# GpSimd's queue issues part and table loads in an attention stage, and the stage's fills stand in another order

## The chip, the core and the metric

The kernel runs on one core of a Trainium2 chip. The core has TensorE (PE; its weight loads are listed as PEld), VectorE (DVE), ScalarE (ACT), GpSimd (POOL) and SyncE (SP), each with an instruction stream of its own. The streams meet only at semaphores. The metric is the device time of one execution in microseconds, median of several; lower is better.

## What is computed

The reference is a network of four layers on x of 16 x 256 tokens with 128 features: linear attention, a mixture of eight experts, disentangled attention, and the experts again. The change touches the third layer, the disentangled attention with 16 heads of 8 features:

```python
scores = jnp.einsum('bhsd,bhkd->bhsk', q, k) / jnp.sqrt(jnp.float32(hd * 3))
c2p = jnp.einsum('bhsd,hkd->bhsk', q, pos_k)
c2p = jnp.take_along_axis(c2p, jnp.clip(rel + span, 0, 2 * span - 1)[None, None], axis=-1)
scores = scores + c2p / bias_scale
p2c = jnp.einsum('bhsd,hkd->bhsk', k, pos_q)
p2c = jnp.take_along_axis(p2c, jnp.clip(-rel + span, 0, 2 * span - 1)[None, None], axis=-1)
scores = scores + p2c.swapaxes(-1, -2) / bias_scale
ctx = jnp.einsum('bhsk,bhkd->bhsd', jax.nn.softmax(scores, axis=-1), v)
```

## The kernel before

`attend` computes this attention. Its work is cut into 32 **units**: one head and one half of the batch (8 entries of 256 x 256 scores). A unit has eight **steps**, one for each batch entry. While a unit's scores are made, the position terms (c2p and p2c) of the next unit are computed too; these are the **fills**, ten for each unit, listed in `FILLS`, and `SHARE` says how many of them stand in each step. Heads 0 and 15 are written out, the 14 between are a loop. I count units from 0 to 31; unit 31 has no fills. Unit 30 loads no tables and no rows, since there is no head 16.

In a step b, in the order of each stream:

- TensorE: `qk` of entry b (L1340), `t2`, the transposes of entry b - 3 (L1351), in the fourth and eighth step `av` (L1362), in the first and fifth `back` (L1369), then the step's fills. Fills: staged ("c2p", L1296, 16 matmul passes), pair (L1332), near (L1323), far (L1305), edge (L1313).
- ScalarE: in the first and fifth step `values` (L1446), then the exponentials of entry b - 3 (L1451), then it copies the step's fills out of PSUM: staged ones by two copies into `STAGE` (L1415), near and edge ones by L1427, pairs by L1434.
- VectorE: the sum of position terms (L1503), the subtraction of the maximum for half of entry b - 1 (L1517), the scores with their maximum (L1510), in the first and fifth step the `results` (L1495, L1498), and the copy of a far fill (L1487).
- GpSimd: the other half of the subtraction (L1266), which `t2` needs too.

A staged fill does not go straight to its place. SyncE copies it from `STAGE` to the tile `CT` by three DMAs, a **spread set** (L1222 twice, L1226 once). `STAGE` holds two fills, so the copy of staged fill 2 waits until the spread set of fill 0 has landed, and fill 3 waits for set 1. VectorE starts a unit when all fills are copied and all four sets have landed.

SyncE also loads for coming units: **parts** (`load_parts`: q once, L1209, k three times, L1211, table ends once, L1212, into a buffer of the next unit; far and edge fills and `qk` read them), **tables** (`load_tables`, L1198, two DMAs) and **rows** (`load_rows`, L1204, 16 small DMAs). The tables and rows loaded in a unit are read by the fills of the next unit. All of it stands in one queue and is issued in the order written. PSUM banks of the fills alternate between two; a fill waits until the fill two banks earlier has been copied out.

## Time and profile before

| | us |
|---|---|
| median of 3 runs | 1508.21 (1508.12 to 1508.65) |
| profiled execution, time | 1508.99 |
| its span, first to last instruction | 1507.0 |
| TensorE / VectorE / ScalarE / GpSimd busy | 1018.8 / 886.6 / 665.2 / 491.6 |
| units, first add of unit 0 to the last score | about 434 to 1293 |

A row of the timeline gives the start in us, the time it took, engine, line, operation, the tiles out<-in, how many instructions are merged, and in brackets how long the engine stood idle before it and what ended the wait. `SPq` is SyncE issuing a DMA; the time in its row is that of the issue, not of the transfer. "granted clock" (PEclk) is TensorE's clock as a share of 2.4 GHz. Busy time of an engine does not bound this stage by itself; what matters is who waits for whom in a unit.

### The profile page before, as it was taken

How to read it: one execution, taken by the hardware profiler on the slowest of the kernel's cores; microseconds unless marked ns; L12 is line 12 of the kernel's file. 1: busy time of each engine (PE TensorE's matmuls, PEld its weight loads, DVE VectorE, ACT ScalarE, POOL GpSimd, SP SyncE). 2: the span in 40 equal slices, each digit the busy share in tenths (PEclk: the TensorE clock that was granted, in tenths of full speed). 3: DMA queues.
4: the chain of work that ended last, by engine and by line, in shares of the span. 5: the costliest groups of instructions: out<-in, count | busy, mean ns of one | idle time of the engine just before them, and what ended most of it. 6: DMA issues, size and time to landing. Idle time of an engine off the chain costs nothing. (4 is left out here: it accounts for less than half of the span.)

```text
span 1507.0 us, 32133 instructions
## 1 busy us (share of the span) xinstructions
PE 1018.8 (68%) x8740; PEld 753.3 (50%) x8740; DVE 886.6 (59%) x2997; ACT 665.2 (44%) x1563; POOL 491.6 (33%) x504
## 2 busy tenths in 40 slices
PE   4892438856257767777677677776777768760876
PEld 3881327754035545455455454554554545560776
DVE  6888635556436656656556555565565656644555
ACT  2237114434435545555455455554554556310443
POOL 3305037531033323323323223232332333203664
PEclk8995559986668988989889889898898999755999
DMA  6900333330765544544444545444454454014331
GB/s 152 212 1 1 126 97 117 95 91 35 270 148 117 122 129 110 128 116 126 123 116 126 123 117 125 116 125 123 111 132 118 119 129 103 1 49 137 103 100 48
DMA packets 113730, 167.21 MB, mean 111 GB/s; under 512 B 16361, under 2 KB 68656, under 8 KB 113168
## 3 DMA queue, kind: packets, MB, share of 16 engines
q1 hardware_dynamic: 108048, 153.93, 40.1%
q0 software_dynamic: 5632, 12.70, 2.4%
q8 instruction: 21, 0.34, 0.1%
q14 instruction: 29, 0.24, 0.1%
HBM read 64.96 MB, written 35.55 MB: 67 GB/s over the span
## 5 line engine op out<-in xcount | busy, mean ns | idle before, releaser
L1266 POOL TENSOR_SCALAR ds_p2c<-ds_p2c,ds_max 128x256 f32<-128x256 f32 x256 | 270.7, 1058 | 576.1 <-DVE ds_max L1510 576.1
L1510 DVE CUSTOM_DVE_ANT_0 ds_p2c<-ds_bank,ds_p2c 128x256 f32<-128x256 f32 x512 | 196.1, 419 | 129.8 <-PE ds_bank L1340 128.9
L1415 ACT ACTIVATE ds_stage<-ds_bank 128x512 f32<-128x512 f32 x256 | 138.9, 595 | 267.4 <-PE ds_bank L1296 142.2
L1296 PE MATMUL ds_bank<-ds_tab,d_qkr 64*64 64x256 f32 x2048 | 176.0, 465 | 57.2 <-DMA d_qkr<-scratch_qk 37.2
L1503 DVE TENSOR_TENSOR ds_p2c<-ds_c2p,ds_p2c 128x512 f32<-128x512 f32 x256 | 184.1, 719 | 42.7 <-ACT ds_p2c L1427 28.6
L1351 PE MATMUL ds_bank<-all_constants,ds_p2c 128*128 128x128 f32 x1024 | 170.8, 293 | 2.9 <-ACT all_xt L1451 1.6
L1451 ACT ACTIVATE all_xt<-ds_bank 128x512 f32<-128x512 f32 x256 | 153.4, 599 | 37.6 <-PE ds_bank L1351 37.4
L1296 PEld LDWEIGHTS ds_bank<-ds_tab,d_qkr 64*64 64x64 f32 x2048 | 101.4, 199 | 105.8 <-issue 76.7
L1351 PEld LDWEIGHTS ds_bank<-all_constants,ds_p2c 128*128 128x128 f32 x1024 | 136.3, 155 | 9.9 <-issue 2.3
L1434 ACT ACTIVATE ds_p2c<-ds_bank 128x256 f32<-128x256 f32 x256 | 77.5, 390 | 114.8 <-PE ds_bank L1332 114.6
L1369 PE MATMUL ds_bank<-all_constants,ds_values_t 128*128 128x128 f32 x128 | 29.4, 313 | 142.1 <-ACT ds_values_t L1446 142.1
L1332 PE MATMUL ds_bank<-d_qkr,ds_tab 64*128 64x128 f32 x1024 | 101.9, 356 | 32.5 <-DVE ds_p2c L1487 32.3
L1517 DVE TENSOR_SCALAR ds_p2c<-ds_p2c,ds_max 128x256 f32<-128x256 f32 x256 | 116.8, 456 | 0.0
L1340 PE MATMUL ds_bank<-ds_ks,ds_qs 72*128 72x256 bf16 x512 | 111.8, 305 | 4.2 <-DVE ds_max L1510 4.2
L1332 PEld LDWEIGHTS ds_bank<-d_qkr,ds_tab 64*128 64x128 f32 x1024 | 86.7, 251 | 52.3 <-DVE ds_p2c L1487 41.0
L1369 PEld LDWEIGHTS ds_bank<-all_constants,ds_values_t 128*128 128x128 f32 x128 | 13.3, 146 | 158.3 <-ACT ds_values_t L1446 158.3
L1487 DVE COPY ds_p2c<-ds_bank 128x512 f32<-128x512 f32 x64 | 44.1, 688 | 75.2 <-PE ds_bank L1305 75.2
L1427 ACT ACTIVATE ds_p2c<-ds_bank 64x512 f32<-64x512 f32 x128 | 75.8, 592 | 28.3 <-PE ds_bank L1313 21.4
L1495 DVE RECIPROCAL ds_rec<-ds_bank 128x8 f32<-128x8 f32 x64 | 13.1, 205 | 119.2 <-PE ds_bank L1369 119.2
L453 ACT ACTIVATE 0fe_h<-0fe_bank,0fe_expert 128x128 f32<-128x128 f32 x160 | 45.6, 368 | 80.0 <-PE 0fe_bank L414 80.0
L453 ACT ACTIVATE 1fe_h<-1fe_bank,1fe_expert 128x128 f32<-128x128 f32 x160 | 45.6, 368 | 79.2 <-PE 1fe_bank L414 79.2
L1340 PEld LDWEIGHTS ds_bank<-ds_ks,ds_qs 72*128 72x128 bf16 x512 | 32.7, 100 | 81.2 <-issue 58.3
(274 smaller groups left out, 1820.0 us busy)
## 6 DMA issues: line engine op xcount, KB each, us to landing
ds_c2p<-ds_stage SPq DMA_DIRECT2D x256, 128.0 KB
ds_c2p<-ds_stage SPq DMA_DIRECT2D x128, 256.0 KB
slots_in<-all_zero SPq DMA_DIRECT2D x2, 5180.0 KB, 38.2
ds_qs<-scratch_q_parts SPq DMA_DIRECT2D x32, 288.0 KB
ds_ks<-scratch_k_parts SPq DMA_DIRECT2D x96, 96.0 KB
d_qkr<-scratch_qk SPq DMA_DIRECT2D x512, 8.0 KB
ds_tab<-scratch_tables SPq DMA_DIRECT2D x32, 248.0 KB, 3.7
ds_tab<-scratch_tables SPq DMA_DIRECT2D x32, 195.5 KB, 3.2
```

The lines of the kernel that those rows point to most:

```text
L453: act.activation(h[i % 2][:, c, :], ph[i % 2][:, c * P:(c + 1) * P], ACT.Gelu_apprx_tanh, bias=WB[i][:, B1_AT + c:B1_AT + c + 1]).then_inc ...
L1266: pool.tensor_scalar(PC[half][:, 1, b, :], PC[half][:, 1, b, :], mx[:, 2 * b + 1:2 * b + 2], None, ALU.subtract).then_inc(s_sub1, 1)
L1296: last = pe.matmul(pc[swap][to * 64:(to + 1) * 64, st * SEQ:(st + 1) * SEQ], own, TAB[half][rows, 0, c:c + SEQ], start=True, stop=True)
L1332: last = pe.matmul(pb[tile][:, :].rearrange("p (r a n) -> p r a n", r=2, a=4)[:, :, a, :], TAB[half][rows, kind, c:c + P], own, start=True ...
L1340: last = pe.matmul(pqk[b % 2][:, st * SEQ:(st + 1) * SEQ], QS[half][:, b * SEQ + st * P:b * SEQ + (st + 1) * P], KS[half][:, b * SEQ:(b + ...
L1351: last = pe.transpose(pt2[:, kt * SEQ + st * P:kt * SEQ + (st + 1) * P], PC[half][:, st, b, kt * P:(kt + 1) * P], con["ident"])
L1415: act.activation(STAGE[:, 2 * (where % 2) + swap, :], pc[swap][:, :], ACT.Copy).then_inc(s_cc, 1)
L1434: last = act.activation(dst, pb[tile][:, side * 256:(side + 1) * 256].rearrange("p (g s b) -> p g b s", g=4, b=HALF), ACT.Copy)
L1451: act.activation(PT[b], pt2[:, :].rearrange("p (k s) -> p k s", k=2), ACT.Exp).then_inc(s_exp, 1)
L1503: dve.tensor_tensor(z, CT[half][:, b, :, :], z, ALU.add).then_inc(s_z, 1)
L1510: last = dve.tensor_tensor_reduce(out=PC[half][:, st, b, :], in0=pqk[b % 2][:, st * SEQ:(st + 1) * SEQ], in1=PC[half][:, st, b, :], scale= ...
L1517: dve.tensor_scalar(PC[half][:, 0, b, :], PC[half][:, 0, b, :], mx[:, 2 * b:2 * b + 1], None, ALU.subtract).then_inc(s_sub0, 1)
```

## The change

Three things. GpSimd's queue issues parts and tables instead of SyncE's: the five part loads after its first subtraction of a unit, the two table loads after its fourth, with the two waits that SyncE had before them; at the start of the stage GpSimd issues the first tables and parts. SyncE's rows are no longer dealt four to each spread set but 5, 0, 9 and 2. And `FILLS` and `SHARE` are changed: staged fills in steps one, two, five and six, a pair in step three, the near fill in step four, a far fill and a pair in step seven, a far fill and the edge fill in step eight. (`own` asks for a semaphore named with the stage's full prefix; `ds` has no digit to strip, so the names stay what they were.)

```diff
-        s_rows, s_ct, s_tab, s_stack = ([m.sem(f"{n}{i}") for i in range(2)] for n in ("rows", "c2p", "tab", "stack"))
+        s_rows, s_ct, s_tab, s_stack = ([m.sem(f"{n}{i}", own=n in ("tab", "stack")) for i in range(2)] for n in ("rows", "c2p", "tab", "stack"))
...
-        FILLS = [CROSS[0], CROSS[1], NEAR, CROSS[2], FARS[0], PAIRS[0], CROSS[3], PAIRS[1], FARS[1], EDGE]
+        FILLS = [CROSS[0], CROSS[1], PAIRS[0], NEAR, CROSS[2], CROSS[3], FARS[0], PAIRS[1], FARS[1], EDGE]
...
-        SHARE = [1, 1, 1, 1, 2, 1, 2, 1]
+        SHARE = [1, 1, 1, 1, 1, 1, 2, 2]
...
-                    if not (last and half == 1):
-                        sp.wait_ge(s_sc, HALF * u + 2)
-                        sp.sem_inc(s_go_sp, 1)
-                        load_parts(*following(head, half))
+                    sp.wait_ge(s_sc, HALF * u + 2)
+                    sp.sem_inc(s_go_sp, 1)
                     if not last:
                         sp.wait_ge(s_bm, BM * (u + 1))
                         sp.sem_inc(s_go_sp, 1)
                         sp.wait_ge(s_cm, CM * (u + 1))
                         sp.sem_inc(s_go_sp, 1)
-                        load_tables(head + 1, half)
-                    for i in range(len(CROSS)):
+                    for i, count in enumerate((5, 0, 9, 2)):
                         if not last:
-                            load_rows(head + 1, half, 4 * i, 4)
+                            load_rows(head + 1, half, (0, 5, 5, 14)[i], count)
                         if not (last and half == 1):
                             spread(*following(head, half), i)
...
                         pool.tensor_scalar(PC[half][:, 1, b, :], PC[half][:, 1, b, :], mx[:, 2 * b + 1:2 * b + 2], None,
                                            ALU.subtract).then_inc(s_sub1, 1)
-
+                        if b == 0 and not (last and half == 1):
+                            load_parts(*following(head, half))
+                        if b == 3 and not last:
+                            pool.wait_ge(s_bm, BM * (u + 1))
+                            pool.sem_inc(s_go_pool, 1)
+                            pool.wait_ge(s_cm, CM * (u + 1))
+                            pool.sem_inc(s_go_pool, 1)
+                            load_tables(head + 1, half)
+
+            load_tables(0, 0)
+            load_parts(0, 0)
+            load_tables(0, 1)
             pool.wait_ge(s_bo, 16)
```

How it moves the instructions, at the three places that matter. First SyncE's queue in the second unit (head 0, second half), before; `ds_qs`, `ds_ks` and `ds_ends` are the parts, `ds_tab` the tables, `d_qkr` the rows, `ds_c2p` the spreads:

```order
L1209 DMA ds_qs<-scratch_q_parts 72x1x2048
L1211 DMA ds_ks<-scratch_k_parts 24x2048 x3
L1212 DMA ds_ends<-scratch_far_f 72x1x256
L1198 DMA ds_tab<-scratch_tables 128x1x391
L1198 DMA ds_tab<-scratch_tables 128x1x496
L1204 DMA d_qkr<-scratch_qk 8x2x128 x4
L1222 DMA ds_c2p<-ds_stage 8x8x512 x2
L1226 DMA ds_c2p<-ds_stage 16x8x512
```

The same queue and unit in the changed kernel:

```order
L1200 DMA d_qkr<-scratch_qk 8x2x128 x5
L1211 DMA ds_c2p<-ds_stage 8x8x512 x2
L1215 DMA ds_c2p<-ds_stage 16x8x512
L1211 DMA ds_c2p<-ds_stage 8x8x512 x2
L1215 DMA ds_c2p<-ds_stage 16x8x512
L1200 DMA d_qkr<-scratch_qk 8x2x128 x9
```

Seven loads no longer stand before the first spread set, and five small row loads do. Next GpSimd's stream in that unit, changed kernel; before, there are eight subtractions in a row here and nothing else:

```order
L1261 TENSOR_SCALAR ds_p2c1<-ds_p2c1,ds_max 128x256 [waits ds_scores]
L1250 DMA ds_qs0<-scratch_q_parts 72x1x2048
L1252 DMA ds_ks0<-scratch_k_parts 24x2048 x3
L1253 DMA ds_ends0<-scratch_far_f 72x1x256
L1261 TENSOR_SCALAR ds_p2c1<-ds_p2c1,ds_max 128x256 [waits ds_scores] x3
L1246 DMA ds_tab1<-scratch_tables 128x1x391 [waits ds_bias_mm,ds_c2p_mm]
L1246 DMA ds_tab1<-scratch_tables 128x1x496
L1261 TENSOR_SCALAR ds_p2c1<-ds_p2c1,ds_max 128x256 [waits ds_scores] x4
```

The second subtraction now stands behind five DMA issues, the fifth behind two more. Last TensorE's stream, fourth to sixth step of the second unit (each step begins with L1340), before:

```order
L1340 MATMUL ds_bank<-ds_ks,ds_qs 128x256 x2
L1351 MATMUL ds_bank<-all_constants,ds_p2c 128x128 x4
L1362 MATMUL ds_bank<-all_xt,ds_head_v 32x256 x8
L1296 MATMUL ds_bank<-ds_tab,d_qkr 64x256 x8
L1340 MATMUL ds_bank<-ds_ks,ds_qs 128x256 x2
L1351 MATMUL ds_bank<-all_constants,ds_p2c 128x128 x4
L1369 MATMUL ds_bank<-all_constants,ds_values_t 128x128 x2
L1305 MATMUL ds_bank<-ds_ks,ds_ends 128x512
L1332 MATMUL ds_bank<-d_qkr,ds_tab 128x2x64 x8
L1340 MATMUL ds_bank<-ds_ks,ds_qs 128x256 x2
L1351 MATMUL ds_bank<-all_constants,ds_p2c 128x128 x4
L1296 MATMUL ds_bank<-ds_tab,d_qkr 64x256 x8
```

and in the changed kernel:

```order
L1346 MATMUL ds_bank<-ds_ks,ds_qs 128x256 x2
L1357 MATMUL ds_bank<-all_constants,ds_p2c 128x128 x4
L1368 MATMUL ds_bank<-all_xt,ds_head_v 32x256 x8
L1329 MATMUL ds_bank<-d_qkr,ds_tab 64x128 x8
L1346 MATMUL ds_bank<-ds_ks,ds_qs 128x256 x2
L1357 MATMUL ds_bank<-all_constants,ds_p2c 128x128 x4
L1375 MATMUL ds_bank<-all_constants,ds_values_t 128x128 x2
L1302 MATMUL ds_bank<-ds_tab,d_qkr 64x256 x8
L1346 MATMUL ds_bank<-ds_ks,ds_qs 128x256 x2
L1357 MATMUL ds_bank<-all_constants,ds_p2c 128x128 x4
L1302 MATMUL ds_bank<-ds_tab,d_qkr 64x256 x8
```

Staged fill 2 (before in the fourth step) moved to the fifth, the far and the pair fill left the fifth step, and the near fill stands in the fourth.

## Rows read from the trace of the kernel before

**Rows 1.** The page, busy time of one engine, its share and instructions.

```profile
PE 1018.8 (68%) x8740; PEld 753.3 (50%) x8740; DVE 886.6 (59%) x2997; ACT 665.2 (44%) x1563; POOL 491.6 (33%) x504
```

**Rows 2.** The list of waits: who waited for whom, us, times, longest.

```profile
ACT ds_stage L1415 <- DMA ds_c2p<-ds_stage: 125.2, 30, 5.0
```

**Rows 3.** The timeline of SyncE's queue, 850 to 905 us.

```profile
872.63 0.87 SPq L1209 DMA_DIRECT2D ds_qs<-scratch_q_parts  x1
...
876.45 1.36 SPq L1198 DMA_DIRECT2D ds_tab<-scratch_tables  x2
878.00 1.79 SPq L1204 DMA_DIRECT2D d_qkr<-scratch_qk  x4
...
881.67 0.58 SPq L1226 DMA_DIRECT2D ds_c2p<-ds_stage  x1
```

**Rows 4.** The timeline of all engines, 881 to 889 us: where they wait.

```profile
885.79 1.08 ACT L1415 ACTIVATE ds_stage<-ds_bank 128x512 f32<-128x512 f32 x2 [4.52 <-DMA ds_c2p<-ds_stage]
...
887.21 0.44 PE L1369 MATMUL ds_bank<-all_constants,ds_values_t 128*128 128x128 f32 x2 [4.05 <-ACT ds_values_t L1446]
...
887.68 0.21 DVE L1495 RECIPROCAL ds_rec<-ds_bank 128x8 f32<-128x8 f32 x1 [4.02 <-PE ds_bank L1369]
```

**Rows 5.** The timeline: first adds of units 0, 1, 30 and 31.

```profile
434.06 0.69 DVE L1503 TENSOR_TENSOR ds_p2c<-ds_c2p,ds_p2c 128x512 f32<-128x512 f32 x1 [5.87 <-DMA ds_c2p<-ds_stage]
...
465.14 0.69 DVE L1503 TENSOR_TENSOR ds_p2c<-ds_c2p,ds_p2c 128x512 f32<-128x512 f32 x1 [1.11 <-DMA ds_c2p<-ds_stage]
...
1255.58 0.69 DVE L1503 TENSOR_TENSOR ds_p2c<-ds_c2p,ds_p2c 128x512 f32<-128x512 f32 x1 [0.95 <-ACT ds_p2c L1427]
...
1277.52 0.69 DVE L1503 TENSOR_TENSOR ds_p2c<-ds_c2p,ds_p2c 128x512 f32<-128x512 f32 x1 [1.11 <-DMA ds_c2p<-ds_stage]
```

**Rows 6.** The timeline of all engines in unit 30, 1253 to 1281 us.

```profile
1256.38 1.16 PE L1296 MATMUL ds_bank<-ds_tab,d_qkr 64*64 64x256 f32 x16
...
1257.46 0.92 POOL L1266 TENSOR_SCALAR ds_p2c<-ds_p2c,ds_max 128x256 f32<-128x256 f32 x1 [1.70 <-DVE ds_max L1510]
...
1258.97 1.16 PE L1296 MATMUL ds_bank<-ds_tab,d_qkr 64*64 64x256 f32 x16 [0.67 <-ACT ds_stage L1415]
...
1260.07 0.39 PE L1340 MATMUL ds_bank<-ds_ks,ds_qs 72*128 72x256 bf16 x2
...
1264.69 0.39 PE L1340 MATMUL ds_bank<-ds_ks,ds_qs 72*128 72x256 bf16 x2
...
1264.98 1.08 ACT L1415 ACTIVATE ds_stage<-ds_bank 128x512 f32<-128x512 f32 x2 [1.33 <-PE ds_bank L1296]
...
1265.61 0.42 DVE L1510 CUSTOM_DVE_ANT_0 ds_p2c<-ds_bank,ds_p2c 128x256 f32<-128x256 f32 x1
...
1266.39 0.44 PE L1369 MATMUL ds_bank<-all_constants,ds_values_t 128*128 128x128 f32 x2 [0.87 <-ACT ds_values_t L1446]
...
1267.25 0.68 DVE L1487 COPY ds_p2c<-ds_bank 128x512 f32<-128x512 f32 x1
...
1268.08 1.16 PE L1332 MATMUL ds_bank<-d_qkr,ds_tab 64*128 64x128 f32 x16 [1.03 <-DVE ds_p2c L1487]
...
1273.33 0.56 SPq L1226 DMA_DIRECT2D ds_c2p<-ds_stage  x1
...
1273.92 0.38 PE L1340 MATMUL ds_bank<-ds_ks,ds_qs 72*128 72x256 bf16 x2
...
1275.67 0.41 PE L1313 MATMUL ds_bank<-ds_ks,ds_ends 72*64 72x512 bf16 x2
```

**Rows 7.** Busy time by stretch: engines in turn, granted clock, DMA share, GB/s.

```profile
861.00:867.00 6.00, 5.63 (x40) 3.86 (x41) 3.05 (x9) 1.90 (x6) 1.19 (x1) 0.50 0.44 101
1255.58:1277.52 21.94, 17.52 (x200) 12.00 (x200) 16.19 (x55) 14.19 (x32) 8.63 (x9) 1.00 0.56 125
```

**Rows 8.** DMA issues on GpSimd: one in the timeline, and L347's min/median/max.

```profile
190.79 0.96 POOL L353 DMA_INDIRECT slots_in<-all_rows,0f_slot  x1 [0.30 <-issue]
...
L347 POOL DMA_INDIRECT tokens<-0fe_y,0fe_token x40: 969/1156/1559, 224.7 to 327.2; - x40
```

More of the change, by code:

```diff
@@ L1195, in _ @@
         def _(sp):
-            def load_tables(head, half):
-                for j in range(2):
-                    sp.dma_start(TAB[half][:, j, 0:(TABLE_Q, TABLE)[j]], views["tables"][j][:, bass.ds(head * DB, DB), :]).then_inc(s_tab[half], 16)
             def load_rows(head, half, first, count):
@@ L1205, in load_rows @@
                                  dram["qk"][:, bass.ds(head * DB, DB), half * HT + at.start:half * HT + at.stop].rearrange("j p n -> p j n")).then_inc(s_rows[half], 16)
-            def load_parts(head, half):
-                rows, cols = bass.ds(head * 3 * DB, 3 * DB), slice(half * HT, (half + 1) * HT)
-                sp.dma_start(QS[half][:, :], views["q_parts"][rows, :, cols]).then_inc(s_stack[half], 16)
-                for i in range(3):
-                    sp.dma_start(KS[half][i * 3 * DB:(i + 1) * 3 * DB, :], views["k_parts"][rows, cols]).then_inc(s_stack[half], 16)
-                sp.dma_start(ENDS[half][:, :], views["far_f"][rows, :, :]).then_inc(s_stack[half], 16)
             def spread(head, half, i):
@@ L1239, in heads @@
                         sp.sem_inc(s_go_sp, 1)
-                        load_tables(head + 1, half)
-                    for i in range(len(CROSS)):
+                    for i, count in enumerate((5, 0, 9, 2)):
                         if not last:
-                            load_rows(head + 1, half, 4 * i, 4)
+                            load_rows(head + 1, half, (0, 5, 5, 14)[i], count)
                         if not (last and half == 1):
                             spread(*following(head, half), i)
-            load_tables(0, 0)
             load_rows(0, 0, 0, 16)
-            load_parts(0, 0)
             for i in range(len(CROSS)):
                 spread(0, 0, i)
-            load_tables(0, 1)
             load_rows(0, 1, 0, 16)
@@ L1260, in _, with load_tables, load_parts @@
         def _(pool):
+            def load_tables(head, half):
+                for j in range(2):
+                    pool.dma_start(TAB[half][:, j, 0:(TABLE_Q, TABLE)[j]], views["tables"][j][:, bass.ds(head * DB, DB), :]).then_inc(s_tab[half], 16)
+            def load_parts(head, half):
+                rows, cols = bass.ds(head * 3 * DB, 3 * DB), slice(half * HT, (half + 1) * HT)
+                pool.dma_start(QS[half][:, :], views["q_parts"][rows, :, cols]).then_inc(s_stack[half], 16)
+                for i in range(3):
+                    pool.dma_start(KS[half][i * 3 * DB:(i + 1) * 3 * DB, :], views["k_parts"][rows, cols]).then_inc(s_stack[half], 16)
+                pool.dma_start(ENDS[half][:, :], views["far_f"][rows, :, :]).then_inc(s_stack[half], 16)
             def heads(head, last):
                 for half in range(2):
+                    u = 2 * head + half
                     for b in range(HALF):
```

## The prediction

> **What bounds the kernel now.** I read the shares first: TensorE is the busiest engine and still idle for a third of the span [rows 1], so the time is in waits. In the list of waits, GpSimd's idle time costs nothing (it is waiting for work); the one that matters is ScalarE's staged copy L1415, which waits 125.2 us in 30 places for a DMA, `ds_c2p<-ds_stage` [rows 2]. Thirty places is once a unit. A unit is eight steps, and its start is best seen at VectorE's first add (L1503): 465.14 for unit 1 and 1255.58 for unit 30, so (1255.58 - 465.14) / 29 = 27.26 us a unit [rows 5].
>
> Then one unit in order of time. SyncE's queue starts it at 872.63 with five loads of parts, two of tables at 876.45 and four of rows at 878.00; only then come the spreads of staged fill 0, the third of them at 881.67 [rows 3]. Staged fill 2 uses the same staging rows, so its copy waits for that landing: it starts at 885.79 after 4.52 us idle. ScalarE takes its work in order, and behind that copy stand `values` and the exponentials; TensorE therefore idles 4.05 us before L1369, VectorE 4.02 us before L1495 [rows 4]. After such a gap TensorE's clock is granted at 0.50 for some microseconds, that is at 1.2 instead of 2.4 GHz [rows 7].
>
> Unit 30 is the trial that the old kernel already holds. SyncE has parts to load there but no tables and no rows. Its staged copy 2 (1264.98) shows no wait, the clock is 1.00 throughout [rows 6, 7], and the unit lasts 1277.52 - 1255.58 = 21.94 us [rows 5], 5.32 us less. The difference of TensorE's waits before L1369 (4.05 against 0.87) explains 3.18 of it [rows 4, 6]; the other 2.14 I put down to the low clock.
>
> **What the change takes from SyncE.** Parts and tables go from 872.63 to 878.00: 5.4 us of SyncE's queue in each unit [rows 3]. What stays is 16 row loads, about 0.43 us each (four and their gaps end at about 879.8), and four spread sets of 2.1 us. Counting from the unit's first add as 0, SyncE is free at -0.9, five row loads end at 1.3, and spread set 0 goes out when its copy is ready, as in unit 30; so no load stands before a spread that is ready. From a set's third DMA to its landing takes 4.1 to 4.2 us (881.67 to 885.79; 1273.33 to 1277.52) [rows 3, 5, 6]. Set 0 lands near 8.5, set 1 near 11.
>
> **What the new fill order does.** Staged copies 2 and 3 come in the fifth and sixth step, the far and edge fills, which need the parts, in the last two. I lay the unit out from the spacings of unit 30 [rows 6], again from its first add. To the fifth step the work is as long as before (a pair fill replaces a near fill and a near fill a staged one: the same size within 0.1 us). L1369 runs at 1266.39 - 1255.58 = 10.8, staged fill 2 at 11.3. From a staged fill to the next, whose bank must be copied out, 1258.97 - 1256.38 = 2.6: fill 3 at 13.9. From there to the next `qk` 1.1 (1258.97 to 1260.07): 15.0. From a `qk` to the end of VectorE's scores 1.3 (1264.69 to 1266.0): 16.3. Only now can VectorE copy the far fill out (0.69, L1487), and the pair fill behind it waits for that bank, as it does at 1268.08: about 17.1. Then `qk` of the last step at 18.2, the edge fill 1.75 later (1273.92 to 1275.67) plus 0.4 for the far fill that now stands before it: 20.35; and from the edge fill to the next unit's first add 1.85 (1275.67 to 1277.52): **22.2 us**. So the new order in itself is no faster than unit 30's; it makes room for late parts.
>
> The last spread set gets little room in this. Staged copy 3 is ready from 15.8; SyncE has two row loads before the set, its third DMA is issued near 17.7 and lands near 21.9, 0.3 us before it is needed. Tables and rows are in flight beside it, so I add 0.3 us.
>
> **What it costs on GpSimd.** No row shows a plain load issued by GpSimd. Bounds: an undisturbed indirect issue takes 0.96 us with 0.30 before it, 1.26 a piece; beside VectorE's copies it takes up to 1.56, with 0.30 that is 1.86 [rows 8]. A plain load has no list of addresses to read and three of the five have only 24 rows, so it could also be cheaper; below 1.26 nothing changes, as follows. GpSimd's first subtraction ends at 1257.46 + 0.92 - 1255.58 = 2.8 [rows 6]. Behind it are now five issues of pitch p, and behind them the subtraction of entry 1, which transpose L1351 needs in the fifth step, at about 9.3 (qk at 9.1). It gets it at 3.9 + 5p, and with the transposes (0.6) and L1369 (0.5) staged fill 2 starts at 5.0 + 5p. The plan above has 11.3. So the unit grows by 5p - 6.3: nothing at p = 1.26, 0.7 at 1.4, 1.7 at 1.6, 3.0 at 1.86. I take p = 1.4, the undisturbed issue plus a third of what the disturbance can add, since VectorE's in-SBUF subtraction fills about that share of a step. The later subtractions have slack again (entry 3 is done near 14, wanted at 15.2), and the two table issues after it (2.8 us) end near 17, with the tables wanted at 23; GpSimd's load is 8.6 us in a unit [rows 7] plus 7 x 1.4 = 18.4 of 23. The waits at the fourth entry (`s_bm`, `s_cm`) count fills of the unit before and are met when they are reached.
>
> **The sum.** 22.2 + 0.7 + 0.3 = 23.2 us a unit against 27.26: 4.06 x 29 units = 118 us. Unit 30 has no stall to lose and gets the GpSimd term, +1. Start and unit 0 (434.06 to 465.14 [rows 5]): tables leave SyncE twice, some 2.5 us, and the five issues stand behind GpSimd's bias add, which costs about as much back; I put -1. The profiled execution took 1508.99 (span 1507.0), 0.8 above the median 1508.21; its parts fit the median to 0.05%. Forecast 1508.2 - 118 = **1390 us**.
>
> **Two rules of the skill.** The rows show SyncE's issues as the cause of the stall. The Trainium skill (DMA: Bandwidth & Descriptors, "Issuing engines are not separate DMA queues") says that a second issuing engine saves only sequencer time, usually small beside the transfer; by that the time stays at 1508, which is rival 4. Unit 30 speaks against it here: 5.32 us follow from issue time.
> The rows show an issue on GpSimd growing from 0.97 to 1.56 us beside VectorE's copies [rows 8]. The Trainium skill (SBUF — State Buffer, "SBUF: two separate sides") says that GpSimd can't write descriptors while VectorE runs a two-port operation; the direction agrees with the trace. What it would do at its full length here is rival 3.
>
> **Rivals.**
> 1. The last spread set decides. It stands 0.3 us from the bound by the plan; if tables, parts and a denser stream of transfers (DMA share 0.56 in unit 30 without tables and rows [rows 7]) delay its landing by 1 to 2 us, the unit is 24.2 to 25.2: 1419 to 1448. For it: spacing; against: the transfers are also spread over two queues. 12 in 100.
> 2. GpSimd is late but the clock stays. Each issue meets one of VectorE's subtractions, p 1.6 to 1.8: unit 24.2 to 25, 1419 to 1443. 8 in 100.
> 3. **Slower: GpSimd late and the clock falls.** TensorE's wait for entry 1 is 3.9 + 5p - 9.3. At p = 1.86 it is 3.9 us, about the gap of 4.05 after which the clock is low today, while the waits of 1.03 in unit 30 left it at 1.00 [rows 4, 6, 7]. The low clock adds 2.1: 22.2 + 3.0 + 2.1 = 27.3, where the kernel is today. Above p = 1.86 it is slower; at 2.2 the unit is 22.2 + 4.7 + 2.1 = 29.0, +50 us, 1559. 6 in 100.
> 4. The change does not do what it says: the stall stays or another of its size takes its place, within 0.2% of 1508. 3 in 100.
> 5. Issues cheap, landing in time: unit 22.0 to 22.4, 1360 to 1367. 8 in 100.
>
> **How the numbers follow.** The forecast's own case, p from 1.26 to 1.6, is a unit of 22.4 to 24.2: 1367 to 1419, 63 in 100. With the faster case and the two late ones the range is 1358 to 1445. 0.2% (3 us) is what a measurement of this kernel can tell. Faster 0.91 (63 + 12 + 8 + 8), within 0.2% 0.03, slower 0.06.
>
> **What the changed profile would show.** Right: a first add every 23 us; no row of L1415 waiting for `ds_c2p<-ds_stage`; granted clock 1.00 through the units; GpSimd issues of 0.9 to 1.3 us, with L1351 waiting under 2 us once a unit. Wrong: waits of L1351 for GpSimd of over 3 us, the clock at 0.50 in each unit, or L1503 waiting for the DMA `ds_c2p<-ds_stage` for over 1 us at each unit's start.

## The result and the profile after

| | before | changed kernel |
|---|---|---|
| median, us | 1508.16 (1507.77 to 1508.65, 4 runs) | 1408.13 (1400.51 to 1416.35, 4 runs) |
| ratio | | 0.9338, 95% interval 0.9277 to 0.9398 |
| span of the profiled execution | 1507.0 | 1410.7 |
| TensorE's granted clock, mean | 0.829 | 0.867 |
| mean of units 1 to 29 | 27.26 | 23.75 |

The kernel is 100 us faster; 118 were forecast. The page's busy line, the answer to [rows 1], shows as many instructions on TensorE and VectorE as before, TensorE done with them sooner since its clock is higher, and 118 us more on GpSimd:

```profile
PE 980.5 (70%) x8740; PEld 719.6 (51%) x8740; DVE 889.5 (63%) x2997; ACT 661.3 (47%) x1563; POOL 610.1 (43%) x728
```

The list of waits (who waited for whom: us, times, longest), the answer to [rows 2]. The staged copy now stands on L1421 and still waits for spread sets, and VectorE's first add of a unit (L1509) waits for them too:

```profile
DVE ds_p2c L1509 <- DMA ds_c2p<-ds_stage: 86.7, 30, 5.1
ACT ds_stage L1421 <- DMA ds_c2p<-ds_stage: 72.6, 28, 4.5
```

First adds of units 0, 1, 8, 9, 16, 17, 30 and 31 in VectorE's timeline, the answer to [rows 5]:

```profile
439.53 0.69 DVE L1509 TENSOR_TENSOR ds_p2c<-ds_c2p,ds_p2c 128x512 f32<-128x512 f32 x1 [2.78 <-DMA ds_c2p<-ds_stage]
...
470.93 0.69 DVE L1509 TENSOR_TENSOR ds_p2c<-ds_c2p,ds_p2c 128x512 f32<-128x512 f32 x1 [4.33 <-DMA ds_c2p<-ds_stage]
...
639.18 0.69 DVE L1509 TENSOR_TENSOR ds_p2c<-ds_c2p,ds_p2c 128x512 f32<-128x512 f32 x1 [1.13 <-DMA ds_c2p<-ds_stage]
...
666.92 0.69 DVE L1509 TENSOR_TENSOR ds_p2c<-ds_c2p,ds_p2c 128x512 f32<-128x512 f32 x1 [1.13 <-ACT ds_p2c L1433]
...
828.85 0.69 DVE L1509 TENSOR_TENSOR ds_p2c<-ds_c2p,ds_p2c 128x512 f32<-128x512 f32 x1 [4.09 <-DMA ds_c2p<-ds_stage]
...
850.94 0.69 DVE L1509 TENSOR_TENSOR ds_p2c<-ds_c2p,ds_p2c 128x512 f32<-128x512 f32 x1 [1.34 <-DMA ds_c2p<-ds_stage]
...
1159.81 0.69 DVE L1509 TENSOR_TENSOR ds_p2c<-ds_c2p,ds_p2c 128x512 f32<-128x512 f32 x1 [1.84 <-DMA ds_c2p<-ds_stage]
...
1181.55 0.69 DVE L1509 TENSOR_TENSOR ds_p2c<-ds_c2p,ds_p2c 128x512 f32<-128x512 f32 x1 [1.84 <-DMA ds_c2p<-ds_stage]
```

The difference of the two traces closes with these rows. Units 1 to 29 take 688.9 us instead of 790.4 (-101.6), unit 0 begins 5.5 us later, unit 0 itself is 0.3 longer, unit 30 is 0.2 shorter, and what follows the start of unit 31 is 0.3 shorter: -96.3, the difference of the spans.

The units are of two kinds, which a mean hides. Eighteen of the 29 take 22.0 to 23.3 us (mean 22.5), unit 16 among them with 850.94 - 828.85 = 22.09. Eleven take 24.3 to 27.7 (mean 25.8), such as unit 8 with 27.74. Had all been of the first kind, the kernel would be 11 x 3.3 = 36 us faster.

Unit 8 in the timelines of SyncE's queue, GpSimd, ScalarE and TensorE, the answer to [rows 3] and [rows 4]:

```profile
641.72 1.28 SPq L1211 DMA_DIRECT2D ds_c2p<-ds_stage  x2
...
642.00 0.62 POOL L1250 DMA_DIRECT2D ds_qs<-scratch_q_parts  x1
...
642.62 1.58 POOL L1252 DMA_DIRECT2D ds_ks<-scratch_k_parts  x3
...
643.18 0.56 SPq L1215 DMA_DIRECT2D ds_c2p<-ds_stage  x1
...
644.16 0.66 POOL L1253 DMA_DIRECT2D ds_ends<-scratch_far_f  x1
...
644.20 2.29 SPq L1211 DMA_DIRECT2D ds_c2p<-ds_stage  x2
...
647.46 4.13 SPq L1200 DMA_DIRECT2D d_qkr<-scratch_qk  x9
...
647.96 1.13 POOL L1246 DMA_DIRECT2D ds_tab<-scratch_tables  x2
...
653.74 1.09 ACT L1421 ACTIVATE ds_stage<-ds_bank 128x512 f32<-128x512 f32 x2 [3.69 <-DMA ds_c2p<-ds_stage]
...
654.97 1.98 PE L1302 MATMUL ds_bank<-ds_tab,d_qkr 64*64 64x256 f32 x16 [3.07 <-ACT ds_stage L1421]
...
657.38 1.08 ACT L1421 ACTIVATE ds_stage<-ds_bank 128x512 f32<-128x512 f32 x2 [2.07 <-DMA ds_c2p<-ds_stage]
```

Spread set 0 is issued beside the parts, set 1 and then the tables and nine rows beside each other. Set 0's third DMA is issued at 643.18 and the copy that waits for it starts at 653.74: 10.6 us, where it was 4.1 before. TensorE waits 3.07 us behind that copy, and its clock falls to 0.50: staged fill 3 takes 1.98 us, the same 16 matmuls 1.16 at full clock [rows 6]. Windows over this stretch (PE, PEld, DVE, ACT and POOL busy, granted clock, DMA share, GB/s) show what the landing met. The DMA share adds up the times of all packets that start in a window, over 16 engines (so a window can pass 1); it stands at 0.81 to 1.07 until set 0 has landed:

```profile
643.00:645.00 2.00, 2.00 (x30) 1.50 (x23) 2.00 (x9) 1.48 (x3) 2.00 (x5) 1.00 0.81 191
645.00:647.00 2.00, 2.00 (x30) 1.11 (x26) 2.00 (x7) 1.79 (x6) 2.00 (x2) 1.00 0.96 163
647.00:649.00 2.00, 1.81 (x26) 1.39 (x22) 1.16 (x5) 0.89 (x2) 2.00 (x4) 1.00 0.93 154
649.00:651.00 2.00, 1.39 (x18) 0.96 (x18) 1.09 (x5) 1.04 (x3) 1.01 (x2) 1.00 1.07 189
651.00:653.00 2.00, 0.90 (x10) 0.58 (x6) 1.90 (x8) 0.00 (x0) 0.38 (x1) 1.00 0.89 184
...
655.00:657.00 2.00, 2.00 (x17) 0.94 (x18) 0.00 (x0) 0.31 (x1) 0.00 (x0) 0.50 0.47 146
```

Before, the ten microseconds from 876 to 886 of unit 16 had a share of 0.56.

What separates the two kinds is the moment at which set 0 leaves. GpSimd issues the parts 2.8 us after a unit's first add (5.5 in unit 17). In seventeen of the eighteen short units set 0's third DMA is out 0.7 to 2.5 us after the first add, ahead of the parts, and by the times at which the trace counts up its semaphore it lands 4.1 to 4.4 us later, as forecast. In the long ones it is out at 3.2 to 4.9 and takes 6.8 to 10.5 us (unit 17: 4.1). Short unit 26 is the border case, 3.1 and 6.9. VectorE's wait at the first add goes with it: 2.1 to 5.1 us in short units, 1.1 to 1.9 in long ones. While VectorE waits there, TensorE and ScalarE get ahead, and set 0 is out sooner after the first add (wait and issue add up to 5.1 us in unit 8 and in unit 16).

### The profile page after: what moved, and what is told of

Its sections match the earlier page's. It is cut to its first block and busy times, and to the rows that moved or that the text cites. A ratio compares the mean times of both kernels' runs of the same rounds, so it can differ in the third digit from the quotient of the medians.

```text
span 1410.7 us, 32238 instructions
## 1 busy us (share of the span) xinstructions
PE 980.5 (70%) x8740; PEld 719.6 (51%) x8740; DVE 889.5 (63%) x2997; ACT 661.3 (47%) x1563; POOL 610.1 (43%) x728
## 5 line engine op out<-in xcount | busy, mean ns | idle before, releaser
L1261 POOL TENSOR_SCALAR ds_p2c<-ds_p2c,ds_max 128x256 f32<-128x256 f32 x256 | 265.9, 1042 | 360.8 <-DVE ds_max L1516 359.7
L1509 DVE TENSOR_TENSOR ds_p2c<-ds_c2p,ds_p2c 128x512 f32<-128x512 f32 x256 | 187.2, 731 | 89.0 <-DMA ds_c2p<-ds_stage 86.7
L1421 ACT ACTIVATE ds_stage<-ds_bank 128x512 f32<-128x512 f32 x256 | 139.0, 595 | 211.3 <-PE ds_bank L1302 138.6
L1302 PE MATMUL ds_bank<-ds_tab,d_qkr 64*64 64x256 f32 x2048 | 156.5, 421 | 88.2 <-ACT ds_stage L1421 51.6
L1357 PE MATMUL ds_bank<-all_constants,ds_p2c 128*128 128x128 f32 x1024 | 164.6, 285 | 9.0 <-ACT all_xt L1457 6.4
L1357 PEld LDWEIGHTS ds_bank<-all_constants,ds_p2c 128*128 128x128 f32 x1024 | 125.4, 148 | 19.8 <-issue 9.7
L1523 DVE TENSOR_SCALAR ds_p2c<-ds_p2c,ds_max 128x256 f32<-128x256 f32 x256 | 114.8, 448 | 0.0
L1346 PE MATMUL ds_bank<-ds_ks,ds_qs 72*128 72x256 bf16 x512 | 105.0, 288 | 11.5 <-DVE ds_max L1516 11.4
L1338 PE MATMUL ds_bank<-d_qkr,ds_tab 64*128 64x128 f32 x1024 | 79.8, 299 | 27.2 <-DVE ds_p2c L1493 27.2
L1338 PEld LDWEIGHTS ds_bank<-d_qkr,ds_tab 64*128 64x128 f32 x1024 | 66.9, 199 | 44.9 <-DVE ds_p2c L1493 33.5
L1368 PE MATMUL ds_bank<-all_xt,ds_head_v 128*32 128x256 f32 x1024 | 77.9, 428 | 0.7 <-ACT all_xt L1457 0.7
L353 POOL DMA_INDIRECT slots_in<-all_rows,1f_slot x32 | 31.6, 986 | 87.7 <-POOLq L176 78.2
L347 POOL DMA_INDIRECT tokens<-0fe_y,0fe_token x40 | 46.3, 1158 | 51.2 <-DVE 0fe_y L485 45.5
```

The costliest lines, as they stand in the source:

```text
L1261: pool.tensor_scalar(PC[half][:, 1, b, :], PC[half][:, 1, b, :], mx[:, 2 * b + 1:2 * b + 2], None, ALU.subtract).then_inc(s_sub1, 1)
L1302: last = pe.matmul(pc[swap][to * 64:(to + 1) * 64, st * SEQ:(st + 1) * SEQ], own, TAB[half][rows, 0, c:c + SEQ], start=True, stop=True)
L1338: last = pe.matmul(pb[tile][:, :].rearrange("p (r a n) -> p r a n", r=2, a=4)[:, :, a, :], TAB[half][rows, kind, c:c + P], own, start=True ...
L1346: last = pe.matmul(pqk[b % 2][:, st * SEQ:(st + 1) * SEQ], QS[half][:, b * SEQ + st * P:b * SEQ + (st + 1) * P], KS[half][:, b * SEQ:(b + ...
L1357: last = pe.transpose(pt2[:, kt * SEQ + st * P:kt * SEQ + (st + 1) * P], PC[half][:, st, b, kt * P:(kt + 1) * P], con["ident"])
L1368: last = pe.matmul(pu[j * VG:(j + 1) * VG, :], VH[half][:, 2 * (4 * part + j) + kt, :], PT[4 * part + j][:, kt, :], start=(kt == 0), stop= ...
```

## The experiments

All times are medians; each ratio is against runs of the kernel before that were taken beside it. "New order" is the changed kernel's `FILLS` and `SHARE`. Of the twelve expectations three held with their range (the rows' deal, staged fill 2 alone, and the last one); the other nine times lie outside every range that was written down for them, so these show directions and not prices.

**One part alone.** First the new order, with SyncE issuing everything as before and the rows dealt four by four:

```diff
-        FILLS = [CROSS[0], CROSS[1], NEAR, CROSS[2], FARS[0], PAIRS[0], CROSS[3], PAIRS[1], FARS[1], EDGE]
+        FILLS = [CROSS[0], CROSS[1], PAIRS[0], NEAR, CROSS[2], CROSS[3], FARS[0], PAIRS[1], FARS[1], EDGE]
-        SHARE = [1, 1, 1, 1, 2, 1, 2, 1]
+        SHARE = [1, 1, 1, 1, 1, 1, 2, 2]
```

> Only the order of the fills and the steps they stand in is changed; SyncE issues parts, tables and rows as before. Theory A (what is left of the stall in the changed kernel is late landings of spread sets, since their transfers share the DMA engines with parts and tables): SyncE's queue still puts set 0 out at 8.1 us of a unit, it lands at 12.3, and staged copy 2 is now wanted only at 12.6, so the old stall goes by the order alone; set 1 lands at 16.3 (wanted 15.1) and set 3 near 24.5, so a unit is 24.8 to 25.3 us, 29 x 2.2 = 64 us less than before, about 1440 to 1450. Rival B (it is the moved issue work that removes the stall, the order alone does little): a unit stays above 26.5, over 1485.

Measured: **1369.1** us, ratio 0.9058 (0.9023 to 0.9094), units of 22.5. That is more than the whole gain of the change: the order alone is 39 us faster than order and queue together. Then the reverse, the changed kernel with the old `FILLS` and `SHARE`:

> GpSimd issues parts and tables and the rows are dealt 5, 0, 9, 2, but the fills stand in the old order. Theory A: staged copy 2 is wanted at 9.4 us of a unit while set 0 lands later than that beside the parts (6 to 10 us after its issue), and the far fill in step five wants parts at 11.3 that land near 14; a unit is 25 to 27 us, 1445 to 1505. Rival B: freeing SyncE's queue is enough, a unit is 22 to 23 as in unit 30, about 1370.

Measured: **1561.6**, ratio 1.0339 (1.0281 to 1.0397): slower than before. Its list of waits has the old stall, only longer (125.2 us in [rows 2]):

```profile
ACT ds_stage L1421 <- DMA ds_c2p<-ds_stage: 168.4, 30, 6.8
```

Both rivals fell with these two: that the moved issue work is what removes the stall, and that freeing SyncE's queue is enough. Theory A comes nearer in both, but it put the new order at least 71 us too slow, and the old one with GpSimd's queue at least 57 us too fast and on the wrong side of the kernel before.

**Issues or bytes.** The changed kernel, with parts of 16 columns and tables of 8 from the second head on: as many DMAs and as many issues, hardly any bytes. The other columns are left out of the computation.

```diff
+                w_, e_ = (HT, 2 * FAR) if first else (16, 16)
-                pool.dma_start(QS[half][:, :], views["q_parts"][rows, :, cols]).then_inc(s_stack[half], 16)
+                pool.dma_start(QS[half][:, 0:w_], views["q_parts"][rows, :, cols]).then_inc(s_stack[half], 16)
```

> The changed kernel, but from the second head on the part and table loads that GpSimd issues carry only the first 8 to 16 columns (same number of DMAs and rows, almost no bytes; later heads compute on stale data). Theory A: with the bytes gone the spread sets land 4 us after their issue, staged copies 2 and 3 wait for no DMA, the low clock goes; the wait of VectorE at a unit's start shrinks from 2.9 to 1 us or less; a unit is 22.3 to 22.8, about 1365 to 1380. Rival C (the price is GpSimd's issue work or the number of its transfers, not their bytes): 23.5 or more, within 10 us of 1408.

Measured: **1346.8**, ratio 0.8931 (0.8903 to 0.8960), units of 21.6. ScalarE's wait for spread sets is gone from the list; one remains:

```profile
DVE ds_p2c L1512 <- DMA ds_c2p<-ds_stage: 64.7, 32, 2.8
```

So the bytes of parts and tables cost the changed kernel 61 us. Their issue on GpSimd costs next to nothing: in this kernel TensorE waited for a subtraction of GpSimd once, 0.6 us, and in the changed kernel never.

**The moment.** Parts after GpSimd's third subtraction instead of the first, tables after the sixth:

> The changed kernel with the parts issued after GpSimd's third subtraction instead of its first, and the tables after the sixth instead of the fourth. Theory A: spread sets 0 and 1 leave alone and land 4 us after issue, no wait of staged copy 2, fewer units with the low clock, a unit 22.5 to 23.2, about 1375 to 1395. Against it: the parts' last load landed 8.9 us after its issue in the changed kernel (median); issued at about 9 it would reach the first far fill, wanted at 15.8, 2 us late, and set 3 meets the tables: 24 to 25 us, 1415 to 1445.

Measured: **1512.7**, ratio 1.0024 (1.0007 to 1.0041). The parts now come too late for the far fill, once in every unit:

```profile
PE ds_bank L1311 <- DMA ds_ends<-scratch_far_f: 103.4, 31, 3.9
```

The other way: GpSimd issues parts and tables ahead of its first subtraction, as soon as SyncE used to:

```diff
+                    pool.wait_ge(s_sc, HALF * u + 2)
+                    if not (last and half == 1):
+                        load_parts(*following(head, half))
+                    if not last:
+                        pool.wait_ge(s_bm, BM * (u + 1))
+                        pool.wait_ge(s_cm, CM * (u + 1))
+                        load_tables(head + 1, half)
                     for b in range(HALF):
...
-                        if b == 0 and not (last and half == 1):
-                            load_parts(*following(head, half))
-                        if b == 3 and not last:
...
-                            load_tables(head + 1, half)
```

> The changed kernel, but GpSimd issues a unit's parts and tables ahead of its first subtraction (parts once two scores of the unit are there, tables right behind), where SyncE issued them, instead of after the first and after the fourth subtraction: parts some 5 us and tables some 8 us earlier, in front of spread sets 0 and 1 rather than beside them. Theory T (the moment: parts and tables fly at the same time as the spread sets): the sets land in 4 to 5 us again, units of 22 to 22.7 us, 1365 to 1380. Theory S (the software queue is itself the slow or greedy one, wherever it is issued): most of the 39 us stay, 1392 to 1415.

Measured: **1354.3**, ratio 0.8986 (0.8962 to 0.9010): the fastest kernel of the study that computes everything, 54 us ahead of the changed kernel, with units of 21.8. It also beats the new order alone, by 15 us, so with the right moment the second queue does pay. Unit 16 in the timelines of GpSimd, VectorE, SyncE's queue and ScalarE:

```profile
792.86 0.64 POOL L1250 DMA_DIRECT2D ds_qs<-scratch_q_parts  x1 [0.31 <-issue]
...
794.79 0.69 DVE L1511 TENSOR_TENSOR ds_p2c<-ds_c2p,ds_p2c 128x512 f32<-128x512 f32 x1 [1.82 <-DMA ds_c2p<-ds_stage]
...
796.15 1.14 POOL L1246 DMA_DIRECT2D ds_tab<-scratch_tables  x2 [0.29 <-PE ds_bank L1304]
...
798.10 0.56 SPq L1215 DMA_DIRECT2D ds_c2p<-ds_stage  x1
...
806.21 1.08 ACT L1423 ACTIVATE ds_stage<-ds_bank 128x512 f32<-128x512 f32 x2 [1.24 <-PE ds_bank L1304]
...
808.70 1.08 ACT L1423 ACTIVATE ds_stage<-ds_bank 128x512 f32<-128x512 f32 x2 [0.92 <-PE ds_bank L1304]
```

The parts leave 1.9 us ahead of the first add and the tables 1.4 us after it, against 2.8 and 8.8 after it in unit 8 of the changed kernel, and set 0, issued at 798.10, has landed when its copy comes at 806.21. Theory T has only half of this. Sets 0 and 1 do not land in 4 to 5 us again: by the semaphores they take 7.0 and 7.8 (medians), since the bytes are still in flight, but in the new order there is room for that. Sets 2 and 3 do, with 4.3 and 4.8 against 6.9 and 6.4 in the changed kernel. Next the tables alone on GpSimd at their late place, the parts back on SyncE:

> The changed kernel with the parts back on SyncE's queue, at the place where it had them; GpSimd issues the tables alone, after its fourth subtraction. Of the 39 us that the new order alone is ahead of the changed kernel: if the parts beside spread set 0 are the cost (1.2 MB a unit, most of what moved), 1368 to 1380; if the tables, which are issued at 8.8 us of a unit beside set 1, are as much to blame, 1385 to 1400; if it is the first loads and the rows' deal, 1400 to 1410.

Measured: **1383.3**, ratio 0.9179 (0.9155 to 0.9202), between the first two cases. (The 1.2 MB of the expectation are wrong: by the page's sizes parts are 0.63 MB a unit, tables 0.45.) And the rows' deal of 5, 0, 9 and 2 on SyncE, new order, no GpSimd:

```diff
-                    for i in range(len(CROSS)):
+                    for i, count in enumerate((5, 0, 9, 2)):
                         if not last:
-                            load_rows(head + 1, half, 4 * i, 4)
+                            load_rows(head + 1, half, (0, 5, 5, 14)[i], count)
```

> The new order on the kernel before (SyncE issues all), with the rows dealt 5, 0, 9 and 2 instead of four before each spread set. Nine rows at 0.42 us are issued between sets 1 and 2: set 2 waits 3.8 us of queue, but its copies come two steps after those of set 1, so it has room; set 1 leaves 1.7 us earlier and copy 3 waits for it 1 us less. The new order alone gave 1369. If the deal costs nothing: 1362 to 1372. If the nine rows push sets 2 and 3 so that the last one lands later at the unit's start: 1375 to 1395, and then the deal is a part of the changed kernel's price.

Measured: **1364.5**, ratio 0.9084 (0.9037 to 0.9131), which can't be told from the 0.9058 of the order with rows dealt four by four. The deal costs nothing. Late tables on GpSimd cost 19 us (1383.3 against 1364.5), the parts there as well another 25 (1408.1), 2.4 of them ahead of unit 0 in the two traces.

**What is left at a unit's start.** With the new order alone VectorE waits 118 us, 32 times, for the last spread set. Staged fills 2 and 3 one step earlier and every set issued ahead of its rows should shorten that:

```diff
-FILLS = [CROSS[0], CROSS[1], PAIRS[0], NEAR, CROSS[2], CROSS[3], FARS[0], ...
+FILLS = [CROSS[0], CROSS[1], PAIRS[0], CROSS[2], CROSS[3], NEAR, FARS[0], ...
```

> The new order on the kernel before, with staged fills 2 and 3 in steps four and five (near in the sixth), and each spread set issued ahead of the rows that stood before it (6, 6, 4, 0 behind sets 0 to 2). If the wait for the last spread set at a unit's start (3.7 us, 32 times with the new order alone) is what bounds it: the last set lands some 3 us earlier, the wait goes down to 1 us or less, units of 20 to 21.3 us, 1300 to 1335. If the staged copies 2 and 3 then wait as much longer for sets 0 and 1: 1360 to 1375.

Measured: **1396.0**, ratio 0.9289 (0.9239 to 0.9339), slower than the order alone. The wait moved to where the old one was:

```profile
ACT ds_stage L1415 <- DMA ds_c2p<-ds_stage: 117.0, 50, 3.8
```

The same order on the fastest kernel, and a variant that moves only staged fill 2:

> GpSimd issues parts and tables early, in the new order (1354), but staged fills 2 and 3 stand in steps four and five and the near fill in step six. The last spread set leaves some 2.7 us earlier; the first addition of a unit waits 1.9 us for it now. If that wait is what is left: units of 20 to 20.8 us, 1305 to 1330. If staged copies 2 and 3 come before sets 0 and 1 have landed, as on SyncE's queue: ScalarE waits 2 us at each, units of 22.5 to 23.5 us, 1380 to 1400.

> As the run beside it, but only staged fill 2 moves up, to step four; near in step five, staged fill 3 in step six as in the new order. Set 2 then lands well ahead of set 3 and shares no DMA time with it. If the last set's landing at the unit's start is long because sets 2 and 3 fly together: the wait of 1.9 us shrinks to about 1, 1325 to 1345. If a single set needs that long anyhow: 1350 to 1360. If copy 2 comes before set 0 has landed: above 1365.

Measured: **1435.9**, ratio 0.9524 (0.9489 to 0.9558), and **1428.9**, ratio 0.9477 (0.9443 to 0.9510), 82 and 75 us behind the kernel that they start from. Copy 2 in step four comes before set 0 has landed: ScalarE waits for spread sets 107 us in the first and 91 in the second, against 5 in the kernel that they start from. ScalarE's timeline of the first:

```profile
820.16 1.08 ACT L1423 ACTIVATE ds_stage<-ds_bank 128x512 f32<-128x512 f32 x2 [3.35 <-DMA ds_c2p<-ds_stage]
...
823.61 1.08 ACT L1423 ACTIVATE ds_stage<-ds_bank 128x512 f32<-128x512 f32 x2 [1.60 <-DMA ds_c2p<-ds_stage]
```

**The relief of SyncE's queue by itself.** The early issue on GpSimd (1354 with the new order), with the old order:

> GpSimd issues parts and tables early, ahead of its first subtraction (with the new order: 1354), but the fills stand in the order of the kernel before. It gives what the relief of SyncE's queue alone is worth, with the bytes out of the spread sets' way. Theory A (as the prediction had it: the old stall at staged copy 2 is SyncE's queue, so taking parts and tables off it lets set 0 leave earlier): copy 2's wait of 4.3 us a unit goes, 1385 to 1420. Theory B (the order is what stalls: copy 2 one step after copy 1 waits for a landing whoever issues, and the pair stands where it cannot be copied in time): 1450 to 1500. If the late issue was not what made the old order with GpSimd's queue slower than before: over 1520.

Measured: **1514.4**, ratio 1.0036 (1.0016 to 1.0056). No gain. SyncE's queue and ScalarE in one unit, first add at 820.48:

```profile
824.48 0.56 SPq L1215 DMA_DIRECT2D ds_c2p<-ds_stage  x1
...
832.29 1.08 ACT L1423 ACTIVATE ds_stage<-ds_bank 128x512 f32<-128x512 f32 x2 [4.07 <-DMA ds_c2p<-ds_stage]
```

Set 0's third DMA is issued 4.0 us after the first add instead of 8.1 (881.67 in [rows 3], in the unit that starts at 873.53). But it takes 7.8 us to its landing instead of 4.1, and the copy starts 11.8 after the first add instead of 12.3. In the median of units 1 to 29 the set is out at 4.0 and lands at 11.9, before at 8.1 and 12.1. The relief worked on the queue and was given back in the landing; the DMA share in this window is 0.87:

```profile
822.00:832.00 10.00, 7.53 (x92) 5.12 (x88) 7.67 (x28) 5.03 (x10) 7.78 (x10) 1.00 0.87 190
```

If the bytes are the reason, the same kernel without them should gain. It leaves out the same columns as the run with few bytes above:

> The fill order of the kernel before, GpSimd issuing parts and tables early (with all bytes: 1514), but from the second head on each part carries 16 columns and each table 8: same transfers, few bytes, other data left out. With all bytes, spread set 0 left SyncE's queue 4.8 us earlier in a unit than before, but took 8 us instead of 4 to land, so staged copy 2 waited as long as before. Theory: landing times are what the bytes in flight make them. Then with few bytes set 0 lands in 4 to 5 us, copy 2 waits for it 1 us or less, and the old order gives units of 22 to 24 us: 1350 to 1415. If the old order stalls in any case (its staged copy 2 comes one step after copy 1, and its pair and far fills stand in two steps): 1450 to 1500.

Measured: **1382.9**, ratio 0.9155 (0.9133 to 0.9178), 131 us less than with all bytes. The same copy, in the unit that starts at 812.34, no longer waits for a DMA:

```profile
816.34 0.56 SPq L1215 DMA_DIRECT2D ds_c2p<-ds_stage  x1
...
821.34 1.09 ACT L1426 ACTIVATE ds_stage<-ds_bank 128x512 f32<-128x512 f32 x2 [1.26 <-PE ds_bank L1307]
```

and the window has a DMA share of 0.39:

```profile
822.00:832.00 10.00, 7.44 (x66) 5.26 (x67) 5.01 (x19) 5.70 (x15) 3.04 (x3) 0.83 0.39 89
```

The corners of the study side by side, medians in us:

| | old order | new order |
|---|---|---|
| SyncE issues all | 1508 | 1369 |
| GpSimd, where the change has it | 1562 | 1408 |
| GpSimd, early | 1514 | 1354 |
| GpSimd, few bytes | 1383 (early) | 1347 (where the change has it) |

Read down, the old order gains nothing from either place on GpSimd as long as the bytes are there. Read across, the new order is worth 139 to 160 us wherever the issues stand, and 36 when landings are fast; that last row compares two places, so its 36 us are rough. Of the 160 us with the early issue, 75 come from asking for set 0 one step later: with staged fill 2 alone moved back to step four they are gone. That variant has its staged fills in steps one, two, four and six, just as the old order has, so the other 85 us (1514 to 1429) come from the other fills' places: near, pair and far, of which a far and a pair fill no longer stand in step five, behind the late copy. Which of these moves is worth what was not taken apart.

How long a spread set takes from its third DMA to its landing, by the semaphore's times, medians of units 1 to 29 in us:

| | set 0 | set 1 | set 2 | set 3 |
|---|---|---|---|---|
| before | 3.9 | 4.0 | 4.1 | 4.0 |
| new order, SyncE issues all | 3.9 | 4.0 | 4.1 | 4.3 |
| changed kernel | 4.2 | 9.2 | 6.9 | 6.4 |
| new order, GpSimd early | 7.0 | 7.8 | 4.3 | 4.8 |
| old order, GpSimd early | 7.9 | 8.4 | 5.3 | 4.0 |
| changed kernel, few bytes | 4.2 | 5.9 | 4.2 | 4.8 |
| old order, early, few bytes | 4.5 | 6.2 | 4.1 | 4.0 |

Set 1 stays near 6 us even with few bytes; it is issued 2.4 us behind set 0 there, 4.2 in the first two rows.

## Why the prediction came out as it did

The forecast was 1390 in a range of 1358 to 1445, and 1408 came. Sign, range and the length of a short unit held. The reason given for them did not, and two errors cancelled: that 1408 lies in the range is luck in part.

**What bounds the kernel.** Right: staged copy 2 waits for spread set 0, and the clock falls behind it.

**What the change takes from SyncE.** This step failed. It took 4.1 to 4.2 us from a set's third DMA to its landing as a constant, since its two rows agreed on it, and concluded that a set issued sooner lands sooner. Both were landings behind a queue that had spaced the loads out. With loads issued beside the sets it measured 7.8 us (early issue, old order), 10.6 (unit 8 of the changed kernel) and 6.6 at a unit's end (844.39, below, to the first add at 850.94). Unit 30 itself spoke against the constant: there set 1's third DMA leaves 6.8 us after the first add and by its semaphore lands at 12.8, 6.1 us later and not "near 11". Used as the trial of relief, that unit was also one for fewer bytes: it has no tables and no rows in flight. The two runs with the old order and the early issue, 1514 with the bytes and 1383 without, show that relief of the queue gains nothing there while the bytes fly beside set 0. They do not show that the bytes alone made unit 30 fast. Before, set 0 landed 3.9 us after an issue at 8.1, so there it was the issue that was late, and the old order needed both, an early issue and a free way. Few bytes with SyncE issuing all was not run.

**What the new fill order does.** "The new order in itself is no faster than unit 30's; it makes room for late parts" is right as a length (22.5 with the order alone, 21.94 in unit 30) and wrong as a role: the order gives more than the whole gain alone (1369), with parts that were not late. The plan's length was near: 22.2 us against 22.09 in unit 16 and 22.5 in the mean of the short units. Its parts were not. Rows of unit 16 of the changed kernel, timelines of TensorE and SyncE's queue, first add at 828.85:

```profile
837.36 0.44 PE L1375 MATMUL ds_bank<-all_constants,ds_values_t 128*128 128x128 f32 x2 [0.75 <-ACT ds_values_t L1452]
837.72 1.16 PE L1302 MATMUL ds_bank<-ds_tab,d_qkr 64*64 64x256 f32 x16
...
844.06 1.16 PE L1338 MATMUL ds_bank<-d_qkr,ds_tab 64*128 64x128 f32 x16 [0.78 <-DVE ds_p2c L1493]
844.39 0.56 SPq L1215 DMA_DIRECT2D ds_c2p<-ds_stage  x1
```

`back` stands at 8.5 where the plan had 10.8, the pair fill at 15.2 (plan 17.1), the last set's third DMA at 15.5 (plan 17.7). The work from the first add on is some 2 us shorter, because TensorE and ScalarE run ahead while VectorE waits for the last set at the unit's start. The landing is 6.6 instead of 4.2, 2.4 us longer. So the plan's "0.3 us before it is needed" is in truth a wait of 4.09 us at the first add, and rival 1's mechanism rules the short units, at the forecast's length. It is also what the prediction had named as a sign that it was wrong: the first add waiting over 1 us at each unit's start. Two of its signs of being right failed as well: L1421, the old L1415, still waits for spread sets (72.6 us), and the clock is not 1.00 throughout (its mean is 0.92 in unit 16 and 0.82 in unit 8).

**What it costs on GpSimd.** The mechanism (five issues between two subtractions) is there; the price is not. One issue, by its line, min, median and max in ns, in the changed kernel:

```profile
L1250 POOL DMA_DIRECT2D ds_qs<-scratch_q_parts x32: 625/625/649, 408.9 to 1162.6; - x32
L1252 POOL DMA_DIRECT2D ds_ks<-scratch_k_parts x96: 509/565/642, 409.5 to 1164.2; - x96
```

They follow each other without a gap, so p is 0.6 and not 1.4, and 5p - 6.3 is below nothing: the term is 0 instead of 0.7. (The 1.4 was not what its reason gives: a third of the way from 1.26 to 1.86 is 1.46, and VectorE's subtraction fills 0.34 to 0.57 us of a step of 2.7 in unit 30, a fifth at most.) An indirect issue was the wrong neighbour to bound a plain load from above; the prediction said that below 1.26 nothing changes, and that held.

**The 0.3 us for transfers beside the last set** is the term that was mis-sized, and it stood at the wrong place. In the eleven long units it is at the staged copies that the sets are late, with the clock behind them: 3.3 us a unit over eleven, 36 us. With 22.5 for all 29 units the span would have been 1375; with the two kinds as measured it is 1411. I had this as rival 1 at 1419 to 1448, but for the last set only.

**Start and unit 0.** Forecast -1, measured +5.8. Of that 2.6 us come from stages ahead of the change, where nothing differs: SyncE's first issue of this stage is at 407.22 instead of 404.66, and at 404.79 in the kernel with the early issue, whose first loads are those of the changed kernel. The rest is the change's. From that issue to the first staged fill it takes 11.5 us (to 418.70), with the early issue 10.9 (to 415.66), and 8.5 before (to 413.20): rows and tables now land beside the parts, all issued at once. With the parts back on SyncE, behind the rows, it takes 8.8 (406.11 to 414.94).

**The two rules of the Trainium skill.** Of the first I wrote that unit 30 speaks against it: "Issuing engines are not separate DMA queues" (DMA: Bandwidth & Descriptors), a second issuing engine saves only sequencer time. With the old order and early issue that is just what was measured, a ratio of 1.0036 for 5.4 us of queue freed in each unit. It is not the whole of it: the queue's time was no small thing there, it was given back in the landings. With the new order the same relief is worth 15 us (1369 to 1354), and with the old order and few bytes early relief and missing bytes together 125 (1508 to 1383). Of the second, GpSimd's descriptors beside two-port operations of VectorE (SBUF — State Buffer, "SBUF: two separate sides"), no run here shows a trace: all 224 issues took 509 to 732 ns, 213 of them beside a busy VectorE, and the 66 beside its subtraction in SBUF (L1523) were no longer than the others. Whether that is a two-port operation no row tells, so this speaks neither for nor against the page.

**Rivals.** Rival 5 had p right but put units of 22.0 to 22.4 at 1360 to 1367; by the sum's own terms 22.0 is 1355. Rival 3, the one that ended slower, needed p above 1.86 and is out by a factor of three. A kernel slower than before did come up, but by another mechanism: the old order with bytes beside set 0 (1562). Parts too late for the far fill gave the gain back and no more (1513, within 0.5% of before).

What stays open: what starts a row of long units in the changed kernel. What keeps the kinds apart can be read (set 0 out ahead of the parts or beside them), and that it takes the bytes at that moment: with few bytes set 0's third DMA is out at 3.2 us, as in a long unit, and lands in 4.2, and all units from 1 to 29 take 21.4 to 21.8. But no run moved set 0 alone past the parts, so that this moment is the cause is argued from one trace and not shown. The runs of the changed kernel differ by 16 us, as many as five long units.

## What to carry to other kernels

A landing time read from a trace belongs to what was in flight with it (3.9 to 10.5 us for the same set here). Before moving loads to a second queue, add up the bytes that will then be issued within one landing, and see whether the waiting transfer is among them: a single queue that delays loads also keeps them apart. First try to ask for the late transfer a step later. If a second queue is then wanted, look for the moment at which bulk loads meet the transfers that have room: issued early here they still made sets 0 and 1 late, but those had a step to spare, and the last set, for which the next unit waits, landed in 4.8 us instead of 6.4.
